# A new order for TensorE's pieces inside an attention unit, and the first state-space batch prepared after the last unit

## The reference, cut to what matters

```
q, k, v = silu(conv4(x @ wq)), silu(conv4(x @ wk)), silu(conv4(x @ wv))     # per head: 128 wide
err = v - k @ proxy_w;  feats = [entropy(x @ unc_w), |err|/|v|, cos(v, v_hat), log1p|err|, head_embed]
beta_fast/slow, lam, amp_fast/slow = sigmoid(heads(silu(silu(feats @ w1) @ w2)))
for each t, for fast and slow:  S = S*g_t;  S += k_t beta_t (v_t - k_t S);  o_t = q_t S
x  = layernorm(x + (lam*o_fast + (1-lam)*o_slow) / rms * onorm_w * sigmoid(g) @ wo)
u  = silu(conv4(in_proj_w @ ctx) + conv_b);  dt, B, C = x_proj_w @ u;  delta = softplus(dt_proj_w @ dt + b)
h_t = h_{t-1} * exp(delta_t * A) + delta_t u_t B_t;  y_t = C_t h_t + D u_t;  x = layernorm(x + y * silu(x))
x  = layernorm(x + ffn_with_experts(x))
```

## Time and profile before

| | |
|---|---|
| median of 3 runs | 4391.4 us (4386.33 to 4396.34) |
| profiled execution | 4410.57 us, span 4408.8 us |
| TensorE matmul busy | 4032.3 us, 91% of the span, 76786 instructions |
| TensorE weight load busy | 2474.8 us, 56% |
| VectorE | 3213.8 us, 73% |
| ScalarE | 2316.9 us, 53% |
| GpSimd | 887.4 us, 20% |
| mean granted TensorE clock | 0.961 |
| attention stage | about 2885 of the 4408.8 us |

### The profile page before, as it was taken

How to read it: one execution, slowest core, us unless ns; L and a number is a source line. 1 busy time by engine, 2 the same in 40 slices (tenths; PEclk the granted TensorE clock), 3 DMA queues, 4 the chain that set the end, 5 groups by cost and what they waited for, 6 DMA issues and landing times. The chain is left out here.

```text
span 4408.8 us, 180329 instructions
## 1 busy us (share of the span) xinstructions
PE 4032.3 (91%) x76786; PEld 2474.8 (56%) x76786; DVE 3213.8 (73%) x5520; ACT 2316.9 (53%) x5803; POOL 887.4 (20%) x1800
## 2 busy tenths in 40 slices
PE   7999999999999999999999999757878769999999
PEld 4666666666666666666666666523333324444443
DVE  4888888888888888888888888469999971212211
ACT  4667676676766667666676666434344331111110
POOL 1323333332333323233232333000000000000000
PEclk8999999999999999999999999778989889999999
DMA  2212222122221212212122221142323323000000
GB/s 74 69 59 64 69 62 69 54 74 60 66 66 57 76 53 72 69 55 76 55 69 64 66 62 54 40 136 79 89 86 92 82 79 132 10 19 29 0 19 10
DMA packets 133581, 277.34 MB, mean 63 GB/s; under 512 B 20860, under 2 KB 62352, under 8 KB 129328
## 3 DMA queue, kind: packets, MB, share of 16 engines
q1 hardware_dynamic: 132640, 265.61, 19.6%
q10 hardware_dynamic: 144, 0.20, 0.0%
HBM read 235.09 MB, written 30.67 MB: 60 GB/s over the span
## 5 line engine op out<-in xcount | busy, mean ns | idle before, releaser
L421 PE MATMUL a_pb<-a_x_t,a_w_qkv 128*128 128x512 f32 x1536 | 839.5, 638 | 17.0 <-DMA a_x_t<-in_x_t 9.0
L1318 DVE TENSOR_TENSOR a_nq<-a_nq,a_tot 128x512 f32<-128x512 f32 (+1 forms) x768 | 491.2, 681 | 121.7 <-PE a_pb L452 81.4
L1280 DVE SCALAR_TENSOR_TENSOR a_acc<-a_pb,a_taps,a_acc 128x511 f32<-128x511 f32 (+2 forms) x576 | 425.5, 739 | 43.9 <-ACT a_acc L864 14.9
L2010 PE MATMUL m_p_y<-m_h,m_ident 128*128 128x512 f32 x512 | 281.2, 701 | 121.5 <-DVE m_h L2208 121.5
L452 PEld LDWEIGHTS a_pb<-a_nq,a_ks 128*32 128x32 f32 x20480 | 212.7, 111 | 208.1 <-issue 144.5
L2476 PE MATMUL f_pb<-f_x_t,f_w_gu 128*128 128x512 f32 x704 | 308.0, 592 | 0.0
L421 PEld LDWEIGHTS a_pb<-a_x_t,a_w_qkv 128*128 128x128 f32 x1536 | 240.2, 191 | 100.3 <-issue 67.9
L452 PE MATMUL a_pb<-a_nq,a_ks 128*32 128x32 f32 x20480 | 250.5, 200 | 49.6 <-DVE a_nq L1309 35.1
L2530 ACT ACTIVATE f_gate<-f_pb 128x512 f32<-128x512 f32 x132 | 78.8, 597 | 410.6 <-PE f_pb L2476 274.3
L2202 DVE TENSOR_TENSOR_SCAN m_h<-m_da,m_h 128x2048 f32<-128x2048 f32 x64 | 283.2, 4424 | 6.9 <-ACT m_da L2131 1.5
L1682 POOL COPY a_apt<-a_apt_fine 32x256 f32<-32x256 f32 x256 | 100.5, 393 | 910.1 <-DVE a_apt_fine L1336 884.6
(11 more groups left out here) (295 smaller groups left out, 8784.0 us busy)
## 6 DMA issues: line engine op xcount, KB each, us to landing
a_rows<-rows SPq DMA_DIRECT2D x192, 512.0 KB, 3.9
a_amp_sums<-amp_sums SPq DMA_DIRECT2D x64, 508.0 KB, 3.7
attn_o<-a_o_t SPq DMA_DIRECT2D x64, 256.0 KB, 2.6
m_b_rows<-ssm_bc SPq DMA_DIRECT2D x64, 256.0 KB, 3.7
m_c_rows<-ssm_bc SPq DMA_DIRECT2D x64, 256.0 KB, 4.5
m_o_t<-attn_o SPq DMA_DIRECT2D x16, 1024.0 KB, 8.6
a_w_qkv<-in_w_qkv SPq DMA_DIRECT2D x48, 256.0 KB, 2.8
f_w_gu<-in_w_gu SPq DMA_DIRECT2D x3, 1536.0 KB, 19.3
```

Source lines behind the costliest of these rows:

```text
L421: mm = nc.tensor.matmul(pb[:, V_BANK if i == P_V else KQ_BANK], w_qkv[:, i, k], x_t[:, k, b * T:(b + 1) * T], start=(k == 0), stop=(k == D ...
L1280: last = nc.vector.scalar_tensor_tensor(acc[:, i, d:T], src[:, 0:T - d], taps[:, i, 3 - d:4 - d], acc[:, i, d:T], ALU.mult, ALU.add)
L1318: last = nc.vector.tensor_tensor(part, part, spread(blocks, list(part.shape)), ALU.mult)
L2010: nc.tensor.matmul(p_y[:, et], ident[:], h[:, (b * DS + n) % 3, et], start=(n == 0), stop=(n == DS - 1), skip_group_check=True).then_inc(s ...
```

## The change

The change has three parts.

1. On TensorE the pieces of a slot stand in another order. The same pieces are there, with the same waits and the same operands.
2. All steps of `ssm_first` move to the slots after the last unit: on TensorE to slots 67 and 68, on ScalarE to the same, on VectorE to 66 and 67. For that `over_units` runs over more slots; where a slot has no piece it writes no instruction.
3. On VectorE `sum_widths(1)` gets an `if` of its own with the same condition, which changes nothing.

The diff, cut to the pieces that matter:

```
-    for n in range(-3, UNITS + 4):
+    for n in range(-6, UNITS + 7):
...
                     if late.has(0):
                         x_fine_sum(late, 1)
-                    if late.has(2):
-                        proxy_v(late)
+                    if late.has(-1):
+                        recur_even(late, 1)
                     if s.n == 0:
                         gate_low(2)
+                    if s.n == UNITS + 3:
+                        ssm_first(0)
+                    if late.has(-3):
+                        gate_logits(late)
+                    if late.has(0):
+                        products(late, 3)
...
                     if late.has(1):
                         turn_rows(late)
+                    if late.has(2):
+                        proxy_v(late)
...
+                    if late.has(3):
+                        project(late, 3, P_V, 2)
+                    if s.n == -1:
+                        gate_low(0)
+                    if late.has(-1):
+                        recur_u(late, 3)
...
                     if late.has(0):
                         x_fine_sum(late, 4)
                     if late.has(3):
-                        project(late, 3, P_V, 2)
+                        project(late, 3, P_V, 3)
...
-                    if s.has(-1):
-                        recur_even(s, 1)
+                    if s.n == UNITS + 3:
+                        ssm_first(FIRST_DT)
+                    if s.n == UNITS + 3:
+                        ssm_first(FIRST_DT + 1)
```

More of the change, by code:

```diff
@@ L726, in slot @@
                         products(late, 3)
+                    if s.n == -1:
+                        unsure(2)
                     if late.has(-1):
@@ L764, in slot @@
                         unsure(3)
+                    if late.has(0):
+                        products(late, 5)
+                    if late.has(3):
+                        project(late, 3, P_K, 1)
+                    if late.has(-1):
+                        recur_u(late, 2)
+                    if late.has(0):
+                        w_fine_sum(late, 3)
+                    if late.has(-1):
+                        recur_odd(late, 2)
                     if late.has(3):
@@ L779, in slot @@
                     if late.has(3):
+                        project(late, 3, P_K, 3)
+                    if late.has(3):
                         project(late, 3, P_V, 0)
-                    if late.has(-1):
-                        recur_u(late, 3)
                     if late.has(0):
@@ L788, in slot @@
                         project(late, 3, P_V, 1)
+                    if late.has(3):
+                        project(late, 3, P_V, 2)
+                    if s.n == -1:
+                        gate_low(0)
+                    if late.has(-1):
+                        recur_u(late, 3)
+                    if s.n == UNITS + 4:
+                        ssm_first(FIRST_DT + 3)
                     if late.has(0):
@@ L791, in slot @@
                     if late.has(3):
-                        project(late, 3, P_V, 2)
+                        project(late, 3, P_V, 3)
+                    if s.n == UNITS + 3:
+                        ssm_first(1)
+                    if s.n == -1:
+                        gate_low(1)
+                    if s.n == -2:
+                        unsure(0)
                     if late.has(-1):
@@ L810, in slot @@
                         project(s, 2, P_Q, 1)
+                    if s.has(2):
+                        project(s, 2, P_Q, 2)
                     if s.has(0):
@@ L814, in slot @@
                         w_64_sum(late)
+                    if late.has(2):
+                        turn_feats(late)
+                    if s.n == UNITS + 3:
+                        ssm_first(2)
                     if s.has(2):
-                        project(s, 2, P_Q, 2)
+                        project(s, 2, P_Q, 3)
+                    if s.n == UNITS + 3:
+                        ssm_first(3)
+                    if late.has(0):
+                        y_64_sum(late)
+                    if s.has(0):
+                        products(s, 1)
+                    if s.has(1):
+                        hidden_1(s)
                     if s.n == 1:
@@ L1145, in slot @@
                         keep_v(late)
-                    if s.n == UNITS + 1:
-                        ssm_first(FIRST_DBL)
                     if late.has(1):
@@ L1249, in slot @@
                         tap(s, 2, P_Q)
-                    if s.n == UNITS - 1:
-                        ssm_first(1)
                     if s.has(1):
                         hide_1(s)
+                    if s.n == UNITS + 3:
+                        ssm_first(2)
+                    if s.n == UNITS + 4:
+                        ssm_first(FIRST_LN)
+                    if s.n == UNITS + 3:
+                        ssm_first(3)
+                    if s.n == UNITS + 3:
+                        ssm_first(FIRST_U)
+                    if s.n == UNITS + 3:
+                        ssm_first(FIRST_DBL)
+                    if s.n == UNITS + 3:
+                        ssm_first(FIRST_DT)
+                    if s.n == UNITS + 3:
+                        ssm_first(FIRST_DT + 1)
+                    if s.n == UNITS + 3:
+                        ssm_first(FIRST_DT + 2)
+                    if s.n == UNITS + 3:
+                        ssm_first(FIRST_DT + 3)
                 def stored_due(s):
@@ L1549, in slot @@
                         decay_nq(late, 5)
+                    if s.n == UNITS + 2:
+                        ssm_first(0)
                     if late.has(-1):
```

101 lines of the change are left out of this document (18 added, 83 removed).

## The result

The changed kernel takes 4521.6 us against 4393.9 us for the kernel before in the same comparison: it is 128 us slower. The ratio, of mean times, is 1.0298, 95% interval 1.0265 to 1.0332. Predicted were 4425 us, 31 to 34 us slower, with 4448 as the upper end. The direction was right, and the forecast cost was a quarter of the real one.

A forecast was written before the change was run, and what follows sets the result against it. TensorE and VectorE were taken to bound a slot in turn. Slots +31, tail +8 and head −5 gave +34 us on the profiled execution's 4410.6, so 4425 against the median of 4391.4, full range 4376 to 4448.

The forecast's parts named there:

- the tail: End of the attention stage, with `ssm_first` behind the last unit: +40 behind M, −32 before it, +8 us.
- the head: Start of the stage: `unsure(0)` fills TensorE's 4.25 us wait for unit 0's convolution, −5 us, from 0 to −8.
- The first new wait: TensorE at the level-3 products would wait some 0.3 us for the level-2 decay, its former cover having moved.
- The second: New TensorE wait of 0.4 us at `turn_rows` for the gate values from GpSimd, until P + 10.5.
- P: The prediction's label for the start of a slot on TensorE; times within the slot count from it.
- no wait at `turn_rows`: Listed sign that the forecast was wrong; the forecast itself had TensorE waiting 0.4 us there for L1644.
- 0.75: Growth in us of a slot without stalls, to 42.42, from the new order on TensorE.
- The longer waits hide more of the 0.94 of stalls: Step for the mean slot: covered stretches grow from 41% to 49%, so 0.25 us of the 0.75 is taken back.
- The term of +0.50 a slot: Net slot cost over 61 slots, 31 us in all, with ends 0 and 46.
- The wait at L452 for L1309: TensorE's wait for level 0's decay at the end of a slot would grow from 0.55 to about 0.9 us.
- M: The last `mean_square`, forecast to come about 32 us earlier (28 to 33.8) without `ssm_first` in the last slots.
- the sum of 53.8: Serial work between M and stage two, 53.8 us where it was 13.7 before.

The follow-up runs named there:

- a_short: The changed kernel with its row transfers cut from the fifth slot on (128 of 1024 columns each): 4477.8 us, 4402.5 for the kernel before.
- a_order: The changed kernel with TensorE's middle, `w_fine_sum` 2 to `x_fine_sum` 4, in the old order, third V projection kept ahead of `x_fine_sum` 4: 4446.8 us, ratio 1.0129 to before.
- a_pv: The changed kernel with the third V projection alone moved back behind `x_fine_sum` 4: 4533.3 us, ratio 1.0311 to the kernel before.
- a_proxy: The changed kernel with `proxy_v` put back ahead of `gate_logits`: 4478.9 us, ratio 1.0182 to the kernel before.
- b_best2: The kernel before with `recur_even` 1 behind `x_fine_sum` 1, head pieces at the changed places and `gram_kq` behind `recur_even` 3: 4391.5 us, ratio 0.9993.
- b_tail: The kernel before with only `ssm_first` moved behind the last unit on all three engines: 4416.5 us, ratio 1.0028.
- a_gram: The changed kernel with `gram_kq` alone moved back behind `w_fine_sum` 3, no longer directly ahead of `x_fine_sum` 3: 4551.2 us, ratio 1.0336 to the kernel before.
- a_even1: The changed kernel with `recur_even` 1 back between products 2 and `x_fine_sum` 1: 4562.3 us, ratio 1.0348 to the kernel before.

## Why the prediction was wrong

Right were the tail and, nearly, the structure of a slot; the head had the right sign. The first new wait is there in a clean slot, 0.42 us at products 3, and 7.2 us in all, 0.13 a slot, where stalls fill the rest. The second, forecast at 0.4, hardly is: TensorE reaches `turn_rows` just when the gate values do (GpSimd ends at 2242.59 + 0.21 = P + 10.41, `turn_rows` starts at P + 10.51), and waits there 2.8 us in all. The prediction had named "no wait at `turn_rows`" as a sign of being wrong; the time P + 10.5 came out all the same, because the pieces ahead of it end about 0.3 later than it had them. The stretch from `turn_rows` to the end of `x_fine_sum` 4 is 21.72 us in a slot without a stall there, 21.59 predicted:

```profile
2200.55 0.61 PE L625 MATMUL a_pb<-a_sum_w,a_vals 128*24 128x255 f32 x2
...
2221.61 0.73 PE L484 MATMUL a_pb<-a_w_fine,a_y_fine 32*32 32x16 f32 x64
```

`grow` 4 on VectorE waits over 1 us, as forecast (the earlier trace rows has 0.33):

```profile
2222.51 0.29 DVE L1345 COPY_PREDICATED a_x_fine<-a_mask_l,a_pb 128x128 f32<-128x128 int32 x1 [1.44 <-PE a_pb L484]
```

The shortest slot with all pieces, from one `mean_square` to the next, grew by 0.6 (41.66 to 42.30); 0.75 was predicted, 46 us over 61 slots.

The step that failed is "The longer waits hide more of the 0.94 of stalls [...] I take 0.25 back, from bounds of 0 and 0.75". It took the stalls as a fixed 0.94 that the order could only hide. The order makes them. Issue time went from 0.65 to 1.88 a slot, and the time at the lower clock from 10 to 44 us, half of which is lost work. By the prediction's stretches, in the mean over 56 slots, with the clean one in brackets:

| stretch | before | changed | a_short | a_order |
|---|---|---|---|---|
| P to `turn_rows` | 11.63 (11.47) | 11.07 (10.51) | 10.95 | 10.93 |
| `turn_rows` to the end of `x_fine_sum` 4 | 20.61 (19.87) | 23.33 (21.72) | 22.29 | 22.03 |
| from there to P | 10.50 (10.33) | 10.23 (10.13) | 10.23 | 10.22 |

The middle one, which TensorE bounds, has no cover for stalls: they take 1.61 us in it where they took 0.74. In the first they take 0.56 for 0.16, although it ends in what was forecast as a covering wait. The term of +0.50 a slot was +1.95 (44.56 for 42.61). The upper bound was wrong for the same reason, because 0 was taken as the worst that the stalls could do. The earlier trace rows shows issue time and the profile's list of queues shows the instruction packets; whether these come in time in the new order was not asked.

Some smaller errors:

- The wait at L452 for L1309 did not grow to 0.9, it stayed at 0.55 a slot (30.7 us in all), and the stretch that ends in it became 0.2 to 0.3 shorter instead of keeping its 10.33.
- The third V projection, +0.96 in the sum, is worth nothing by itself (a_pv), and `proxy_v` 0.85 and not 0.68 (a_proxy), so that the 0.75 is near the measured 0.6 partly by luck.
- The head's −7.7 was −5 in the sum: the wait of 4.25 is gone from the trace and one of 1.3 at L594 has come, but the first P of the other kernels with this head lies anywhere from 132.9 to 140.7 (143.3 in b_best2), so the size is not settled.
- M came 28.4 us earlier by its distance from unit 62's P, 30.4 in b_tail, 31.6 in a_order, all within 28 to 33.8.
- Behind M the sum of 53.8 met 54.4 by two errors that cancel in part: the first tap comes at M + 5.0 and not 6.6, and the matmuls take 23.7 us and not 21.0.
- The formula of the Trainium skill that the prediction used, on the page "TensorE: Matmul & The Clock Gate", section "Back-to-back issue gap", is there the gap of an isolated matmul; for a stream the same section counts the weight load too, so it does not say that an order changes no spacing. It was worth little either way.
- For the clock in the tail the same page of the Trainium skill, section "What's actually happening", has an idle TensorE at 1.2 GHz, and that pointed the right way: the last two blocks of `ssm_first` take 3.78 us for four passes each, at a granted clock of 0.50 (2972 to 2978 us), the lower level.

**Open.** Touching pieces alone don't make the stalls of the middle (a_gram, b_best2), nor are they gone with later transfers (a_proxy, whose `turn_rows` is later, keeps 34.2 us at the same two pieces and the `w_fine_sum` before them). That every kernel with the new middle has both the quick 299 entries and the late packets points at the quickness, but no run changed it alone. What holds a packet back when the row transfers are cut is not known either: in a_short it starts 3.7 us after its 299 entries begin, 6 to 8 us behind `mean_square`. That the 1.4 us are the time to take a block up was read from the gaps, no run changed it. What instruction supply costs in the quiet stretch is shown only as stalls, whose removal (a_even1) met another wait.

## What to carry to other kernels

Where an engine runs through hundreds of instructions in a few microseconds, its instructions are a stream of DMA packets that can come late. Look for issue time in the middle of a piece, and for what the DMA engines do there. Before a reorder of short instructions, compare which transfers run beside them, and don't take the stalls of the old order as a constant. Measure how fast the engine runs through the entries of one packet in the old order and in the new one. A stall ahead of a wait costs little, one in the stretch that its engine bounds is paid, and a long one is paid again at the lower clock.

## What the runs showed of the hardware that was not expected

- TensorE's instructions come in packets of 16,384 bytes for 256 entries, 611 in this program, and practically all of TensorE's unexplained idle time (104.3 of 104.5 us) lies where a new packet begins. TensorE stood still for 2.23 us (until 427.19) for a packet that started during a row transfer of 512 KB.
- Two extra transfers of 512 KB a slot that nobody reads, at a time when no row transfer runs, made the kernel 0.9% slower (b_load). The stage's row transfers cut to an eighth made it 0.7% faster (b_short).
- After the stall of 2.23 us the granted clock was 0.54 for 3.66 us, though TensorE was busy throughout.
